# Expert offsets packed for TensorE, clamped-source edges joined ahead of the edge loop, routing of the last lap moved

## The reference: what is computed

```
a_src, a_dst = sum(h * att_src), sum(h * att_dst)        # 4 heads of 4 experts
e     = leaky_relu(a_src[src] + a_dst[dst], 0.2)          # 262144 edges, and one loop per node
ee    = exp(e - segment_max(e, dst)[dst])
agg   = segment_sum(h[src] * ee / segment_sum(ee, dst)[dst], dst) + b_gat
score = mean over heads of layernorm(agg)
w     = softmax(top 2 of the 4 scores)
out   = sum over the experts of w[e] * (gelu(x W1[e] + b1[e]) W2[e] + b2[e])
```

## Time and profile before

| | |
|---|---|
| median of 3 runs | 1541.07 us (1539.52 to 1543.46) |
| the profiled execution | 1543.47 us, of which the span of its instructions is 1541.6 |
| DVE busy | 1119.1 us (73%) |
| POOL busy | 873.8 us (57%) |
| PE busy | 863.4 us (56%), weight loads 681.7 us (44%) |
| ACT busy | 453.7 us (29%) |
| mean granted TensorE clock | 0.624 of 2.4 GHz |

### The profile page before, as it was taken

The page is one execution under the profiler, slowest core; times in us unless marked ns, Lnnn a source line. Parts: engine busy times, 40 slices in busy tenths (PEclk is TensorE's granted clock), DMA queues, the critical chain, the costliest instruction groups (busy, mean ns, idle before and its releaser), DMA issues.

```text
span 1541.6 us, 36854 instructions
## 1 busy us (share of the span) xinstructions
PE 863.4 (56%) x13362; PEld 681.7 (44%) x13362; DVE 1119.1 (73%) x2726; ACT 453.7 (29%) x813; POOL 873.8 (57%) x891
## 2 busy tenths in 40 slices
PE   0322332348888882654599975666566455644430
PEld 0222322237777772654233434565456445544430
DVE  6999899876676664896866646666666456788878
ACT  0232232224444444673233321222122112222110
POOL 0045565546666662000477777777777777777750
PEclk9955555557666665776699985555555555555555
DMA  7100000022221124000300000000010000011101
GB/s 165 22 21 21 25 28 28 28 55 52 50 51 49 48 56 144 2 29 13 30 10 10 10 11 10 12 12 12 12 12 14 12 12 12 12 16 20 24 9 27
DMA packets 82063, 45.73 MB, mean 30 GB/s; under 512 B 59719, under 2 KB 75887, under 8 KB 81650
## 3 DMA queue, kind: packets, MB, share of 16 engines
q1 hardware_dynamic: 52210, 22.36, 6.6%
q0 software_dynamic: 27632, 19.12, 6.5%
q10 hardware_dynamic: 2064, 2.10, 0.7%
HBM read 28.10 MB, written 15.93 MB: 29 GB/s over the span
## 4 chain that ended last, share of the span: by engine, by line
POOL 36%; issue 12%; DVE 3%; DMA 1%; POOLq 0%; PE 0%; SPq 0%; ACT 0%; DVEq 0%
POOL edges_rows L338 36%; DVE all_stack L2225 1%; DMA table<-edges_rows 1%; DVE all_stack L2227 0%; DMA edges_ub<-in_L_ffn_b_dram 0%; POOLq L76 0%; DVE all_x_sb L2228 0%; DVE all_x_sb L2229 0%; DMA edges_rows<-table,edges_src 0%; DVE edges_work L1930 0%; PE edges_acc L2471 0%; DVE edges_work L1926 0%; DVE edges_as_sb L1933 0%; DVE all_ad_sb L1933 0%; POOL edges_krow L338 0%
## 5 line engine op out<-in xcount | busy, mean ns | idle before, releaser
L338 POOL DMA_INDIRECT edges_rows<-table,edges_src x576 | 564.6, 980 | 175.6 <-issue 175.6
L194 DVE TENSOR_TENSOR sorting_keys<-sorting_keys 128x512 f32<-128x512 f32 (+2 forms) x370 | 209.7, 608 | 15.6 <-ACT sorting_keys L319 11.9
L732 POOL DMA_INDIRECT y_rows<-mixture_yt,mixture_xin x144 | 156.6, 1087 | 103.2 <-ACT mixture_yt L954 80.5
L727 POOL DMA_INDIRECT x_rows<-mixture_sent,mixture_slot x128 | 139.5, 1090 | 126.6 <-DVE mixture_slot L787 88.1
L2538 ACT ACTIVATE edges_hotT<-edges_h 128x1024 bf16<-128x1024 bf16 x72 | 69.8, 1021 | 307.8 <-PE edges_h L2433 307.8
L1067 PE MATMUL mixture_bank<-mixture_xT,sorting_w_part 128*128 128x128 bf16 x864 | 112.1, 260 | 30.5 <-ACT mixture_xT L940 12.4
L1067 PEld LDWEIGHTS mixture_bank<-mixture_xT,sorting_w_part 128*128 x864 | 87.0, 107 | 57.0 <-issue 44.8
L2490 PE MATMUL edges_acc<-edges_term_parts,edges_work 128*128 128x20 bf16 x1728 | 51.6, 179 | 100.6 <-DVE edges_term_parts L1854 100.6
L2490 PEld LDWEIGHTS edges_acc<-edges_term_parts,edges_work 128*128 128x128 bf16 x1728 | 49.1, 104 | 108.0 <-issue 108.0
L2471 PE MATMUL edges_acc<-edges_end_parts,edges_work 128*128 128x4 bf16 x1728 | 51.1, 166 | 50.8 <-DVE edges_end_parts L1854 50.8
L872 DVE TENSOR_TENSOR mixture_hidden<-mixture_gated,mixture_bank 128x256 f32<-128x256 f32 x72 | 30.1, 419 | 65.5 <-PE mixture_turned L1076 31.4
(11 more groups left out here) (478 smaller groups left out, 2194.1 us busy)
## 6 DMA issues: line engine op xcount, KB each, us to landing
edges_rows<-table,edges_src POOLq DMA_INDIRECT x576, 2.4
mixture_xin<-x_rows SPq DMA_DIRECT2D x144, 49.0 KB, 1.8
all_eo<-y_rows SPq DMA_DIRECT2D x6, 512.0 KB, 6.7
y_rows<-mixture_yt,mixture_xin POOLq DMA_INDIRECT x144, 2.6
sorting_w<-in_L_ffn_w_dram SPq DMA_DIRECT2D x4, 512.0 KB, 8.4
x_rows<-mixture_sent,mixture_slot POOLq DMA_INDIRECT x128, 2.3
out_dram<-all_x_sb SPq DMA_DIRECT2D x8, 256.0 KB
constants_src_i<-in_L_ffn_edge_index_dram SPq DMA_DIRECT2D x1, 1024.0 KB, 5.0
```

The source lines that it names most:

```text
L194: self.st.mark(dve.tensor_tensor(target[half], source[0], source[1], (ALU.min, ALU.max)[half]))
L338: pool.indirect_dma_start(to, None, rows, where).then_inc(done, 16)
L727: pool.indirect_dma_start(x_rows, bass.IndirectOffsetOnAxis(ap=slot[g % 2][:, c, t:t + 1], axis=0), now[c][:, t, :], None).then_inc(scatte ...
L732: pool.indirect_dma_start(y_rows, bass.IndirectOffsetOnAxis(ap=xin[j % XB][:, ROWX - 2:ROWX - 1].bitcast(U32), axis=0), yt[j % YB][:, :], ...
```

## The change

In `mixture` DVE makes one number per pair of tiles, second offset times 2048 plus first offset. PE loads that number without a check of bounds, takes the two offsets from it with a mask and a shift, and holds each in a register. In `graph` the clamped-source edges are joined into `tops` and `sums` for all 64 tiles at once, ahead of the stray loop and the edge loop; `route_gaps` and the first half of `route_totals` are gone. In the last lap `route_totals` stays in the first turn of a group's successor, `route_scores` moves to the end of that turn, the gate (`route_gate`) and the first image to the next turn, and the second image to the start of the turn after it, ahead of that turn's wait for its rows. ACT's root moves behind the exponentials of the first turn.

```diff
@@ -855,6 +858,10 @@
             dve.tensor_copy(maps[0:1, :], maps_ps[0:1, :]).then_inc(maps_ready, 1)
+            dve.wait_ge(maps_ready, 1)
+            both = maps[0:1, 2 * P:4 * P].rearrange("a (n two) -> a n two", two=2)
+            dve.scalar_tensor_tensor(pair_experts[0:1, :], both[:, :, 1], float(PACK), both[:, :, 0], ALU.mult, ALU.add)\
+                .then_inc(pairs_ready, 1)
             while sort.stage < sort.STAGES[0]:
@@ -1033,7 +1040,7 @@
             pe.wait_ge(weights.loaded, 80)
-            pe.wait_ge(maps_ready, 1)
+            pe.wait_ge(pairs_ready, 1)
@@ -1050,11 +1057,11 @@
             def load_experts(pair):
-                for j in (2 * pair, 2 * pair + 1):
-                    load_expert(j)
-            def load_expert(j):
-                experts[j] = pe.value_load(maps[0:1, 2 * P + j:2 * P + j + 1], min_val=0, max_val=(K - 1) * H)
+                both = pe.value_load(pair_experts[0:1, pair:pair + 1])
+                for half, offset in enumerate((both & (PACK - 1), both >> (PACK.bit_length() - 1))):
+                    experts[2 * pair + half] = pe.snap(offset.with_bounds(min_val=0, max_val=(K - 1) * H))
@@ -2054,7 +2060,9 @@
             add_bias(FFN_GROUPS - 1)
-            done = st.n
+            dve.wait_ge(last_in, 16)
+            st.link(dve.tensor_tensor(shared, last_row[:, Q:ROW].unsqueeze(1).to_broadcast([P, T, HEADS]), ad_sb[:, :, :], ALU.add))
+            st.link(dve.scalar_tensor_tensor(shared, shared, 0.2, shared, ALU.mult, ALU.max))
@@ -2073,7 +2081,29 @@
             dve.wait_ge(times_read, 1)
-            st.mark(dve.tensor_scalar(absent[:, :], times[:, :], 0.0, NONE, ALU.is_le, ALU.mult))
+            st.link(dve.tensor_scalar(absent[:, :], times[:, :], 0.0, NONE, ALU.is_le, ALU.mult))
+            def four(v):
+                return v.rearrange("p (t h) -> p t h", h=HEADS)
+            def five(v):
+                return v.rearrange("p t (h k) -> p t h k", h=HEADS)
+            def each(v):
+                return v.unsqueeze(3).to_broadcast([P, T, HEADS, NE + 1])
+            st.link(dve.tensor_tensor(shared, shared, per_channel(absent[:, :], HEADS), ALU.add))
+            st.link(dve.tensor_tensor(joint, tops[:, :, :], shared, ALU.max))
+            st.mark(dve.tensor_tensor(four(gaps[:, 0, :]), tops[:, :, :], joint, ALU.subtract))
+            st.link(dve.tensor_tensor(four(gaps[:, 1, :]), shared, joint, ALU.subtract))
+            dve.sem_inc(gaps_ready, 1)
+            st.mark(dve.tensor_copy(tops[:, :, :], joint))
+            dve.wait_ge(exps_ready, 1)
+            st.mark(dve.tensor_tensor(five(sums[:, :, :]), five(sums[:, :, :]), each(four(exps[:, 0, :])), ALU.mult))
+            st.link(dve.tensor_tensor(four(exps[:, 1, :]), four(exps[:, 1, :]), per_channel(times[:, :], HEADS), ALU.mult))
+            st.link(dve.tensor_tensor(five(last_part), five(last_row[:, 0:Q].unsqueeze(1).to_broadcast([P, T, Q])),
+                                      each(four(exps[:, 1, :])), ALU.mult))
+            st.link(dve.tensor_tensor(sums[:, :, :], sums[:, :, :], last_part, ALU.add))
@@ -2156,36 +2186,17 @@
-            def route_gaps(q):
+            def route_totals(q):
                 if q == 0:
-                    dve.wait_ge(last_in, 16)
                     dve.wait_ge(vec_in, 48)
...
                         rt.mark(dve.memset(order[:, k:k + 1], float(NE - k)))
-                now = tiles(q)
-                rt.link(dve.tensor_tensor(shared, last_row[:, Q:ROW].unsqueeze(1).to_broadcast([P, TP, HEADS]), ad_sb[:, now, :], ALU.add))
-                rt.link(dve.scalar_tensor_tensor(shared, shared, 0.2, shared, ALU.mult, ALU.max))
-                rt.link(dve.tensor_tensor(shared, shared, per_channel(absent[:, now], HEADS), ALU.add))
-                rt.link(dve.tensor_tensor(top, tops[:, now, :], shared, ALU.max))
-                rt.mark(dve.tensor_tensor(gaps[:, 0, :, :], tops[:, now, :], top, ALU.subtract))
-                gaps_marks[q] = rt.n
-                dve.tensor_tensor(gaps[:, 1, :, :], shared, top, ALU.subtract).then_inc(gaps_ready, 1)
-            def route_totals(q):
-                now = tiles(q)
-                dve.wait_ge(exps_ready, q + 1)
-                rt.mark(dve.tensor_tensor(by_head(total), by_head(sums[:, now, :]), wide(exps[:, 0, :, :], NE + 1), ALU.mult))
-                rt.link(dve.tensor_tensor(exps[:, 1, :, :], exps[:, 1, :, :], per_channel(times[:, now], HEADS), ALU.mult))
-                rt.link(dve.tensor_tensor(by_head(part3), by_head(last_row[:, 0:Q].unsqueeze(1).to_broadcast([P, TP, Q])),
-                                          wide(exps[:, 1, :, :], NE + 1), ALU.mult))
-                rt.link(dve.tensor_tensor(total, total, part3, ALU.add))
-                rt.link(dve.tensor_scalar(inverse, by_head(total)[:, :, :, 0], 1e-16, None, ALU.add))
+                total = by_head(sums[:, tiles(q), :])
+                rt.link(dve.tensor_scalar(inverse, total[:, :, :, 0], 1e-16, None, ALU.add))
                 rt.link(dve.reciprocal(inverse, inverse))
-                rt.link(dve.tensor_tensor(by_head(agg), by_head(total)[:, :, :, 1:NE + 1], wide(inverse, NE), ALU.mult))
+                rt.link(dve.tensor_tensor(by_head(agg), total[:, :, :, 1:NE + 1], wide(inverse, NE), ALU.mult))
                 rt.link(dve.tensor_tensor(agg, agg, vector(0), ALU.add))
@@ -2209,17 +2220,20 @@
-            def route_image(q, half=0):
-                if half == 0:
-                    dve.wait_ge(gap2_exp_ready, q + 1)
-                    rt.link(dve.tensor_scalar(shares[1], gap2_exp, 1.0, None, ALU.add))
-                    rt.link(dve.reciprocal(shares[0], shares[1]))
-                    rt.link(dve.tensor_tensor(shares[1], shares[0], gap2_exp, ALU.mult))
-                    rt.mark(dve.tensor_tensor(masks[0], masks[0], per_channel(shares[0], NE), ALU.mult))
-                    rt.link(dve.tensor_tensor(masks[1], masks[1], per_channel(shares[1], NE), ALU.mult))
-                    rt.link(dve.tensor_tensor(gate, masks[0], masks[1], ALU.add))
+            def route_gate(q):
+                dve.wait_ge(gap2_exp_ready, q + 1)
+                rt.link(dve.tensor_scalar(shares[1], gap2_exp, 1.0, None, ALU.add))
+                rt.link(dve.reciprocal(shares[0], shares[1]))
+                rt.link(dve.tensor_tensor(shares[1], shares[0], gap2_exp, ALU.mult))
+                rt.mark(dve.tensor_tensor(masks[0], masks[0], per_channel(shares[0], NE), ALU.mult))
+                rt.link(dve.tensor_tensor(masks[1], masks[1], per_channel(shares[1], NE), ALU.mult))
+                rt.link(dve.tensor_tensor(gate, masks[0], masks[1], ALU.add))
+            def route_image(q, half):
@@ -2244,6 +2258,8 @@
                         mine = rows[:, u, tiles(g), :]
+                        if final and s >= LAP and s % LAP == LAP - 1:
+                            route_image(done, 1)
                         dve.wait_ge(side_ready, at(s))
@@ -2252,8 +2268,6 @@
                             add_sums(s - 1)
-                        if final and s >= LAP and s % LAP == 0:
-                            route_gaps(done)
                         if not first and not final:
@@ -2290,8 +2304,10 @@
                         st.mark(dve.tensor_copy(old, now[:, :]))
-                        if final and s >= LAP:
-                            (route_totals, route_scores, route_image)[s % LAP](done)
+                        if final and s >= LAP and s % LAP == 0:
+                            route_totals(done)
+                        if final and s >= LAP and s % LAP == 1:
+                            route_gate(done)
                         dve.wait_ge(now_ready, at(s))
@@ -2306,8 +2322,10 @@
                         split(dve, st, term_parts, term[:, :], term[:, :], term_parts_ready)
-                        if final and s >= LAP and s % LAP == LAP - 1:
-                            route_image(done, 1)
+                        if final and s >= LAP and s % LAP == 0:
+                            route_scores(done)
+                        if final and s >= LAP and s % LAP == 1:
+                            route_image(done, 0)
                         if s == SEQ - 1:
@@ -2317,10 +2335,10 @@
             join_lap(last_lap, Steps(dve, final_steps), group_major, final=True)
-            route_gaps(GROUPS - 1)
             route_totals(GROUPS - 1)
             route_scores(GROUPS - 1)
-            route_image(GROUPS - 1)
+            route_gate(GROUPS - 1)
+            route_image(GROUPS - 1, 0)
             route_image(GROUPS - 1, 1)
@@ -2521,6 +2539,8 @@
             strays = act.value_load(starts.turns_i[0:1, 3:4], min_val=1, max_val=SC)
+            act.wait_ge(gaps_ready, 1)
+            act.activation(exps, gaps, ACT.Exp).then_inc(exps_ready, 1)
             with act.Fori(0, strays) as c:
@@ -2569,15 +2584,11 @@
                 done = s // LAP - 1
-                if done >= 0:
-                    if s % LAP == 0:
-                        route_exps(done)
```

(23 more changed lines are left out.)

## The result

The changed kernel takes 1487.47 us (median of 4 runs, 1486.66 to 1490.26), the kernel before beside it 1541.61. The ratio is 0.9651 with a 95% interval of 0.9639 to 0.9663: 54 us faster. I had forecast 1507 and a range of 1496 to 1524, so the direction was right and the size was not: 20 us more came than I had counted, and the time lies outside the range.

What follows compares the result with a forecast made beforehand. It took the expert stage's pair cycle to go round through PE's sequencer, and POOL's gathers to pace the graph stage. -28 + 0.3 - 6.5 = -34 us, from the 1541.07 median to 1507, range 1496 to 1524.

Steps and rivals of the forecast that it cites:

- Part 1: Expert stage: packed offsets save 0.55 us per pair, only where PE has a hole ahead of `hide`; sum 28 us.
- My sign: Expert stage, PE: holes ahead of `hide` mostly below 0.1 us, with cycles of about 2.95 us.
- What was late next: Expert stage after packing: POOL's two scatters need 2.77 us per pair, then the array 2.8 at the 1.2 GHz level.
- The rival with the full saving: Expert stage: closed holes let the 2.4 GHz level cover more, saving the full 0.7 per pair; 1497 us, chance 0.15.
- dear arithmetic: Expert stage: mask, shift and holds cost like four 151-ns operations, saving 0.08 to 0.2 per pair; 1525 us, chance 0.13.
- take over: Expert stage: DVE's sorting and products fill the shorter cycles, so half of the saving goes; 1521 us, chance 0.06.
- The rival on the slow side: Expert stage: denser DVE work pushes all POOL's scatters to 1.467 us, so the kernel ends slower; 1548 us, chance 0.06.
- Part 2: Graph stage: joining ahead of the loop costs DVE 8.8 us, hidden in its middle-lap wait of 15.1, becoming about 9.
- The contention: Ahead of the graph loop: three 1280-element DVE operations stretch POOL's gathers by 1 to 3.7 us, taken as plus 3.
- Part 3: Last lap: turn 11 loses gate and images, minus 8.2 us; tail loses gap and joining instructions, minus 3.5.
- Its later start: Last lap: turn 11 starts 5.2 us later, through DVE's moved routing and rows delayed by POOL's 3 and 1.9.
- Parts 2 and 3: Graph stage routing together: 5.2 - 8.2 - 3.5 = -6.5 us; about -9.6 if POOL's stalls vanished.

Runs made afterwards that it cites:

- the run with fewer scatters: The changed kernel with every fourth tile's outputs not scattered (36 of 144), that output left out: 1480.61 us, 6.9 less than the changed kernel.
- the run of the routing alone: The kernel before with all of the change in the graph block but still two checked loads per pair: 1531.73 us, ratio 0.9933.
- the packed offsets alone: The kernel before with only the packed offsets of the change, its routing as before: 1497.52 us, ratio 0.9715.
- the pieces: The changed kernel with an image's weighting in four pieces of 512 elements, the last group's left whole: 1488.16 us, ratio 0.9654.

## Why the prediction was wrong, step by step

**Part 1, the step that failed:** "The saving counts only where there is a hole ... Cut at 0.55 each they give 32 us." Two things in it. The count: the cycle was the sequencer's in all 72 pairs, those without a hole too, which the loads' starts in the trace of before would have told me (above). I had written that the cycle "goes round through PE's sequencer", and then priced it by the array's idleness. My sign that the holes would be mostly below 0.1 us didn't come either: 42 of 72 are longer in the changed kernel, and its cycle is still 0.64 shorter, where I had 0.45 (2.95). The size: 0.55 per pair was 0.79, beyond the 0.71 that I had as the upper end, because the mask and the shift cost 0.13 and the one register operation that I had to go by 0.21. 72 x 0.79 = 57 us are what the sequencer gave, and the stage's last scatter came 43.7 earlier. Of the 13 between them I had taken off 1 for POOL; the run with fewer scatters gives 6.9 back, and for the rest the cause stays open. The first gather starts 43.3 earlier, where I had 27.7: the stage's share of the miss is 16 of the 20 us.

**What was late next** was named rightly: "POOL, then the array itself". POOL's 2.77 per pair became the bound. The rival with the full saving put the stage's end at POOL's 548 and the time at 1497; the stage ended at 546. Its stage came nearest, for a wrong reason, the clock, and I gave it 0.15. Of the other rivals, dear arithmetic fell with the 0.13 us, and VectorE didn't take over: it still idles 30.9 us ahead of `hidden`.

**POOL's scatters did not slow down** with denser sorting: 1.085 after 1.087. The rival on the slow side fell there.

**Part 2** held where it mattered: VectorE's instructions (8.8 forecast) came out of the wait, 15.1 to 6.7, 8.4 less. The contention was mis-sized, plus 1.4 instead of 3. From the timeline of after, VectorE's three long instructions and POOL's gathers beside them:

```profile
882.45 1.49 DVE L2102 TENSOR_TENSOR all_sums<-all_sums,all_stack 128x1280 f32<-128x1280 f32 x1 [0.31 <-ACT all_stack L2543]
...
884.31 1.49 DVE L2104 TENSOR_TENSOR all_stack<-edges_last_row,all_stack 128x1280 f32<-128x1280 f32 x1
885.84 1.49 DVE L2106 TENSOR_TENSOR all_sums<-all_sums,all_stack 128x1280 f32<-128x1280 f32 x1
```

```profile
883.28 1.49 POOL L338 DMA_INDIRECT edges_rows<-table,edges_src  x1 [0.31 <-issue]
885.07 1.55 POOL L338 DMA_INDIRECT edges_rows<-table,edges_src  x1 [0.30 <-issue]
886.93 1.22 POOL L338 DMA_INDIRECT edges_rows<-table,edges_src  x1 [0.30 <-issue]
```

Three gathers of 0.95 grew by 0.54, 0.60 and 0.27, near the lower of the two rows that I had (1.31 in the earlier trace rows). Instructions of the same length took 1.24 from a gather there and much less here, which no run explains; I had taken nearly the upper row for all three.

**Part 3:** turn 11 minus 8.1 (forecast 8.2), the tail minus 3.5 (3.5). Its later start was 1.8 instead of 5.2, and only 0.6 in the run of the routing alone: the forecast had POOL 4.9 late there, and it is 1.9 late in the one trace and 0.7 in the other. (Differences of this size aren't told between single traces: with the packed offsets alone, where the graph block is that of before, the gathers take 737.9 us, and before 740.2.) I had counted the stall of an image at its new place and not taken off those that there were the earlier trace rows: in the trace of before four images run beside gathers, which lose 7.0 us by it, in that of after six, and the loss is again 7.0. Parts 2 and 3 came to 9.4 instead of 6.5.

That such instructions stretch gathers at all is borne out, in these rows and by the pieces. By the Trainium skill's inference that they leave descriptor generation alone ("SBUF — State Buffer", section "Who interferes with whom") parts 2 and 3 would have stood at -9.6, and -9.4 came. The agreement is luck, since the stalls that were to vanish are there: the three gathers above lost 1.4 us, and turn 11 still starts on rows. Whether what was held is the making of descriptors or another part of the gather, no run here shows.

## What to carry to other kernels

When a stage repeats, read the distance from start to start of one instruction across pairs that differ (with and without extra work, with a hole and without): if it doesn't change, what sets it is not the engine whose idleness one was about to count. Then price the change over every repetition, and stop it at the next resource's own total. Register loads on a sequencer are part of that total: the check of a load cost 0.29 us here, the load itself 0.36.

## What the runs showed of the hardware

- TensorE's clock can rise without the time falling: 0.66 to 0.97 in the expert stage, with four transposes more per pair, and 1543.9 us after 1542.0.
- Four more transposes lengthened the cycle of the pairs by no more than 0.02 us: 3.42 after 3.40.
- An image's weighting in four instructions of 512 elements took 2.49 us, whole 2.29. Beside the whole ones a gather of 0.95 took up to 2.86 us, beside the pieces no more than 1.23.
